# Graph attention kernel: a row bent by VectorE before one exponential, first-row steps inside the leftover loop, minus x in earlier batches

## What is computed

```
s = HW @ a[:OUT_F, 0]
t = HW @ a[OUT_F:, 0]
e = jax.nn.leaky_relu(s[row] + t[col], negative_slope=ALPHA)
m = jax.ops.segment_max(e, row, num_segments=N_NODES)
ex = jnp.exp(e - m[row])
den = jax.ops.segment_sum(ex, row, num_segments=N_NODES)
att = ex / den[row]
agg = jax.ops.segment_sum(att[:, None] * h[col], row, num_segments=N_NODES)
```

## Time and profile before

| | us |
|---|---|
| median of 3 runs | 394.81 |
| the 3 runs | 394.67, 394.81, 396.28 |
| profiled execution, its own time | 394.77 |
| its span | 393.0 |

### The profile page before, as it was taken

The page is one execution under the profiler, slowest core; times in us unless marked ns, Lnnn a source line. Parts: engine busy times, 40 slices in busy tenths (PEclk is TensorE's granted clock), DMA queues, the critical chain, the costliest instruction groups (busy, mean ns, idle before and its releaser), DMA issues.

```text
span 393.0 us, 5049 instructions
## 1 busy us (share of the span) xinstructions
PE 379.8 (97%) x1888; PEld 299.6 (76%) x1888; DVE 346.1 (88%) x438; ACT 261.4 (67%) x251; POOL 35.3 (9%) x88
## 2 busy tenths in 40 slices
PE   5999979999999999999999999999999999999994
PEld 2556647888888888778888888888888888888883
DVE  8999989986787698999899999889999899989445
ACT  1569964755566879865786766777758686866222
POOL 5000310000000001001010101001010101001000
PEclk9999999999999999999999999999999999999999
DMA  7900891000000036549545464623423453633202
GB/s 251 391 16 2 141 274 62 3 0 0 2 0 2 0 108 224 151 127 322 167 123 182 124 166 156 203 66 89 127 60 100 130 170 128 224 92 87 75 27 101
DMA packets 23482, 45.90 MB, mean 117 GB/s; under 512 B 1862, under 2 KB 2074, under 8 KB 23458
## 3 DMA queue, kind: packets, MB, share of 16 engines
q0 software_dynamic: 12400, 24.00, 23.2%
q1 hardware_dynamic: 11058, 21.58, 16.4%
HBM read 43.02 MB, written 2.56 MB: 116 GB/s over the span
## 4 chain that ended last, share of the span: by engine, by line
PE 90%; ACT 5%; DMA 2%; DVE 1%; issue 1%; SPq 0%; DVEq 0%
PE PS L1237 63%; PE PS L1177 17%; PE PS L1115 3%; PE PS L1158 3%; DMA av<-in_a 2%; ACT C L857 2%; PE PS L1045 1%; PE PS L1187 1%; ACT xl L884 1%; ACT Z L862 1%; PE PS L1063 1%; PE PS L1101 1%; PE PS L1095 0%; ACT strow L850 0%; ACT ex L902 0%
## 5 line engine op out<-in xcount | busy, mean ns | idle before, releaser
L1237 PE MATMUL PS<-wh,s 128*128 128x512 f32 x720 | 222.8, 390 | 0.4 <-issue 0.4
L1237 PEld LDWEIGHTS PS<-wh,s 128*128 128x128 f32 x720 | 135.1, 188 | 29.7 <-issue 1.8
L1237 PE MATMUL PS<-wl,s 128*128 128x512 f32 x360 | 140.1, 389 | 0.0
L1237 PEld LDWEIGHTS PS<-wl,s 128*128 128x128 f32 x360 | 67.6, 188 | 13.9
L966 ACT ACTIVATE s<-v 128x1280 fp32r<-128x1280 f32 (+1 forms) x32 | 40.0, 1251 | 40.6 <-DVE v L775 23.8
L949 ACT ACTIVATE v<-xt,bias 128x1280 f32<-128x1280 f32 (+1 forms) x32 | 42.9, 1340 | 20.1 <-DVE s L785 18.7
L769 DVE SCALAR_TENSOR_TENSOR v<-v,v 128x1280 f32<-128x1280 f32 (+1 forms) x32 | 46.4, 1450 | 6.3 <-ACT v L952 6.3
L775 DVE SCALAR_TENSOR_TENSOR v<-v,v 128x1280 f32<-128x1280 f32 (+1 forms) x32 | 46.8, 1461 | 3.7 <-DVE v L771 0.5
L785 DVE SCALAR_TENSOR_TENSOR s<-v,s 128x1280 fp32r<-128x1280 f32 (+1 forms) x32 | 46.5, 1454 | 2.4 <-ACT s L966 2.4
L425 POOL DMA_DIRECT2D wh<-in_splT x32 | 22.9, 715 | 272.2 <-PE PS L1237 172.5
L771 DVE SCALAR_TENSOR_TENSOR v<-v,v 128x1280 f32<-128x1280 f32 (+1 forms) x32 | 46.5, 1453 | 0.0
(11 more groups left out here) (141 smaller groups left out, 347.8 us busy)
## 6 DMA issues: line engine op xcount, KB each, us to landing
wh<-in_splT POOLq DMA_DIRECT2D x32, 512.0 KB, 4.2
wring<-in_splT SPq DMA_DIRECT2D x21, 512.0 KB, 4.0
xt<-in_xT SPq DMA_DIRECT2D x1, 2500.0 KB, 12.3
xh<-in_x POOLq DMA_DIRECT2D x1, 2304.0 KB, 11.6
out<-xr SPq DMA_DIRECT2D x9, 256.0 KB
wh<-in_baseT POOLq DMA_DIRECT2D x4, 512.0 KB, 5.2
xl<-in_x POOLq DMA_DIRECT2D x1, 1536.0 KB, 11.9
wring<-in_baseT SPq DMA_DIRECT2D x3, 512.0 KB, 4.6
```

The lines of the kernel that those rows point to most:

```text
L1237: m = e.matmul(PS[:, w % 8, :], sx[:, ic, tl * 128:tl * 128 + 128], wx[:, ic, :], start=first and n == 0, stop=last and n == 2)
```

## The change

Four things are changed.

1. **One exponential per row tile.** ACT writes a new tile `gentle`, 0.2 times `trow`, once (`e.mul`, ahead of all exponentials). Of the two exponentials and the maximum behind them, DVE now takes the maximum first: `bent(j)` is the greater of `gentle - s_part` and `trow`, in one instruction per row; ACT then takes one exponential of it in place (`grow`), and `weigh` is the product with `C` alone. `small` has three one-column instructions, the first two of which do not wait for each other.
2. **Steps moved into the loop's body.** The marks of windows 22 to 24 are split: row tiles 0 and 1 (`NEAR`) inside the loop, ahead of the addition to `C`; the other eight behind `weigh(1)`. The second part of row tile 0's greatest value and `bent(0, 0)` stand in the body as well. The wait for `top` moves from the end of the body to the start of a turn and to the instruction behind the loop.
3. **Minus x** is written in batches 6 to 15, not 8 to 17.
4. **Orders.** On DVE `greatest(1)` goes behind both pieces of row tile 0's `weigh`, and each `bent(j)` stands between `greatest(j)` and `small(j)`, up to j = 3; from 4 on it stands behind `p_low(j - 2)`. PE's zero matmuls are 6 and 2 in place of 8, 4, 4 and 2, and both turns of row tile 0 stand ahead of its sums.

```diff
-        NEGATIVE_AT = {8 + k: k for k in range(NT)}
+        NEGATIVE_AT = {6 + k: k for k in range(NT)}
-        MARKED, MARKED_AHEAD = 20, 22
+        MARKED, MARKED_AHEAD, NEAR = 20, 22, 2
...
+            e.memset(top[:, 0:LW], -BIG).then_inc(s_touch, 1)
...
+            def bent(j, p=0):
+
+                lo, hi = pieces(j)[p]
+                if j >= 3:
+                    e.wait_ge(s_t, upto(j - 3, len(pieces(j - 3)) - 1))
+                e.wait_ge(s_trow, 3)
+                e.wait_ge(s_scol, 3)
+                e.wait_ge(s_gentle, 1)
+                return e.scalar_tensor_tensor(out=ex[:, j % 3, lo:hi], in0=gentle[:, lo:hi], scalar=s_part[:, j:j + 1],
+                                              in1=trow[:, lo:hi], op0=ALU.subtract, op1=ALU.max)
...
+                    e.wait_ge(s_touch, n + 1)
                     greatest_of(0, slice(0, DW * MARKED), LW).then_inc(s_early, 1)
                     e.wait_ge(s_cnt, taken(MARKED_AHEAD - 1))
                     marks(MARKED, MARKED_AHEAD).then_inc(s_ahead, 1)
+                    e.wait_ge(s_cnt, len(TAKEN))
+                    marks(MARKED_AHEAD, ND, 0, NEAR).then_inc(s_near, 1)
...
+                    greatest_of(0, slice(DW * MARKED, N), LW + 1).then_inc(s_late, 1)
                     e.wait_ge(s_ova, n + 1)
+                    e.wait_ge(s_late, n + 1)
...
-                    e.wait_ge(s_touch, n + 1)
-            marks(MARKED_AHEAD, ND).then_inc(s_marked, 1)
-            e.wait_ge(s_marked, 1)
+                    bent(0, 0).then_inc(s_first, 1)
...
-                e.wait_ge(s_e1, n)
-                e.wait_ge(s_e2, n)
-                e.tensor_tensor(b, b, ex[:, 3, lo:hi], ALU.max).then_inc(s_top, 1)
-                e.wait_ge(s_top, n)
+                e.wait_ge(s_ex, upto(j, p))
...
             small(0)
+            bent(0, 1).then_inc(s_z, 1)
+            weigh(0, 0)
+            weigh(0, 1)
             greatest(1)
-            weigh(0, 0)
+            bent(1).then_inc(s_z, 1)
             small(1)
-            weigh(0, 1)
             p_low(0, 0)
+            p_low(0, 1)
+            weigh(1)
+            marks(MARKED_AHEAD, ND, NEAR, NT).then_inc(s_marked, 1)
+            e.wait_ge(s_marked, 1)
             greatest(2)
...
+            def grow(j, p=0):
...
+                e.wait_ge(s_small, smalls(j + 1))
+                e.activation(b, b, ACT.Exp, bias=sm[:, 1, j:j + 1]).then_inc(s_ex, 1)
...
+            e.mul(gentle[:, :], trow[:, 0:N], SLOPE).then_inc(s_gentle, 1)
```

More of the change, by code:

```diff
@@ L186, in build @@
         s_setup = sem("s_setup")
-        (s_reach, s_bits, s_col, s_mk, s_bound, s_left, s_tab, s_mv, s_head, s_ovk, s_ovm, s_ovs, s_ova, s_ovz, s_marked, s_ahead, s_early, s_touch, s_late, s_tmax, s_small, s_top, s_p, s_den, s_rden, s_plo,
+        (s_reach, s_bits, s_col, s_mk, s_bound, s_left, s_tab, s_mv, s_head, s_ovk, s_ovm, s_ovs, s_ova, s_ovz, s_marked, s_ahead, s_early, s_near, s_touch, s_first, s_late, s_tmax, s_small, s_z, s_p, s_den, s_rden, s_plo,
          s_a3, s_b3, s_spl, s_slo, s_wlo, s_res, s_bns, s_bna, s_rstd, s_nb, s_fin) = (
             sem(f"v_{n}") for n in (
-                "reach", "bits", "col", "mk", "bound", "left", "tab", "mv", "head", "ovk", "ovm", "ovs", "ova", "ovz", "marked", "ahead", "early", "touch", "late", "tmax", "small", "top", "p", "den", "rden", "plo",
+                "reach", "bits", "col", "mk", "bound", "left", "tab", "mv", "head", "ovk", "ovm", "ovs", "ova", "ovz", "marked", "ahead", "early", "near", "touch", "first", "late", "tmax", "small", "z", "p", "den", "rden", "plo",
                 "a3", "b3", "spl", "slo", "wlo", "res", "bns", "bna", "rstd", "nb", "fin"))
-        (s_lk, s_sq, s_neg, s_war, s_wa, s_srow, s_trow, s_scol, s_cnt, s_hole, s_e1, s_e2, s_phi, s_ya, s_ev, s_abs, s_q2, s_a2,
+        (s_lk, s_sq, s_neg, s_war, s_wa, s_srow, s_trow, s_scol, s_cnt, s_hole, s_gentle, s_ex, s_phi, s_ya, s_ev, s_abs, s_q2, s_a2,
          s_silu, s_shi, s_root, s_fina) = (sem(f"a_{n}") for n in (
-             "lk", "sq", "neg", "war", "wa", "srow", "trow", "scol", "cnt", "hole", "e1", "e2", "phi", "ya", "ev", "abs", "q2", "a2",
+             "lk", "sq", "neg", "war", "wa", "srow", "trow", "scol", "cnt", "hole", "gentle", "ex", "phi", "ya", "ev", "abs", "q2", "a2",
              "silu", "shi", "root", "fina"))
@@ L600, in _ @@
                     e.wait_ge(s_tab, TABLE)
-                    first, tiles, first_win, many = (
-                        within(v, *ends) for v, ends in zip(loaded(e, r_size, 0, 4, 0, LND * NC), (
-                            (0, NC), (1, NC + 1), (0, LND - 1), (1, LND))))
+                    first, tiles, first_win, many, left = (
+                        within(v, *ends) for v, ends in zip(loaded(e, r_size, 0, 5, 0, LND * NC), (
+                            (0, NC), (1, NC + 1), (0, LND - 1), (1, LND), (1, LND * NC))))
             def greatest_of(j, d, k):
@@ L670, in greatest @@
                 if j == 0:
-                    greatest_of(0, slice(DW * MARKED, N), LW + 1).then_inc(s_late, 1)
-                    e.wait_ge(s_late, 1)
+                    e.wait_ge(s_touch, left + 1)
                     e.tensor_reduce(tmax[:, 0:1], top[:, :], AX.X, ALU.max).then_inc(s_tmax, 1)
@@ L746, in _ @@
             inverse(2)
+            greatest(3)
+            bent(3).then_inc(s_z, 1)
             small(3)
@@ L751, in _ @@
                 p_low(j + 1)
+                if j + 3 < NT:
+                    bent(j + 3).then_inc(s_z, 1)
                 if j + 2 < NT:
@@ L979, in scale @@
                                  ).then_inc(s_fina, 1)
-            for p in range(2):
-                e1(0, p)
-                e2(0, p)
+            e.wait_ge(s_trow, 3)
+            e.mul(gentle[:, :], trow[:, 0:N], SLOPE).then_inc(s_gentle, 1)
+            grow(0, 0)
+            grow(0, 1)
             p_high(0, 0)
-            e1(1)
-            e2(1)
             p_high(0, 1)
+            grow(1)
             p_high(1)
-            e1(2)
-            e2(2)
+            grow(2)
             normalise(0)
-            e1(3)
+            grow(3)
             for j in range(1, NT - 1):
@@ L1192, in _ @@
             e.wait_ge(s_tmax, 1)
[L1193 to L1197 removed]
+            keep_warm(6)
+            e.wait_ge(s_ex, 1)
+            keep_warm(2)
             turn(0, 0)
[L1199 removed]
+            turn(0, 1)
             sums(0, 0, 0)
[L1201 removed]
             sums(0, 2, 0)
@@ L1204, in _ @@
             sums(0, 2, 1)
+            sums(0, 1, 0)
             turn(1)
-            sums(0, 1, 0)
             sums(0, 1, 1)
```

58 lines of the change are left out of this document (18 added, 40 removed).

## The result

| us | kernel before | changed kernel |
|---|---|---|
| runs beside each other | 11, median 394.97 (394.64 to 396.4) | 11, median 394.05 (394.0 to 394.63) |
| ratio | | 0.9968, 95% interval 0.9956 to 0.998 |
| the profiled execution, its own time | 394.77 | 394.55 |
| its span | 393.0 | 392.7 |

The forecast was 393.7, with a range of 392.6 to 395.1 and "within 0.5%" at 0.85. The time came in the range and in that class, 0.35 above the forecast. A gain of 0.9 stands against a forecast of 1.05, but it is not made of what the prediction said.

A forecast was written before the change was run, and what follows sets the result against it. DVE's work in the handoff from counting to row tiles was taken to hold PE: 0.58 of DVE plus 0.47 that was to spare gave 1.05, so 394.77 - 1.05 = 393.7, with 8 in 10 between 392.6 and 395.1.

The forecast's parts named there:

- within 0.5%: Whole kernel: a time within about 2.0 us of no change, between 392.8 and 396.8, chance 0.85.
- What bounds: Handoff from counting to row tiles, 46 to 60 us: DVE is late, not ACT; PE later waits for row tile 2's ph.
- Minus x: gain nil: Last counts: ACT ready about 0.7 earlier, but two row tiles' marks take the place of DVE's 0.31 wait; addition near 48.63.
- The loop's body: Steps up to tmax: the 0.43 of branches runs beside bent(0, 0), so tmax starts at 50.72 instead of 51.30, gain 0.58.
- DVE's stretch from `tmax` to row tile 3's bias: DVE's list after tmax: added and removed steps sum to +0.1 or nothing, so 20.1 us again and the bias at 70.8.
- From the bias to the exponential: ACT at row tile 3: bias before at 71.4, exponential from 71.45; now the bias comes 0.58 earlier, at 70.8.
- From the exponential to PE: Exponential 1.25, copy 1.21, ph at 73.3; PE starts sums(2, 0) at 73.3 to 73.4, not 74.38: gain 1.05.
- PE ahead: Row tile 0: PE idles 1.75 before tmax, transposes at 52.9 and 54.1, 3.0 us ahead; 1.9 turns into a wait.
- The clock at nothing: Handoff: with fewer zero matmuls the granted clock still holds, as through the longer pause before; cost nothing.
- The rival's own reckoning: Clock falls in the handoff: PE has about 0.9 in hand before the gain suffers; 395.8, up to 400, chance 0.06.
- The 0.40 at 161.87 moves with PE: Near the end of the row tiles: PE's 0.40 us break hangs on row tile 9's ACT and DVE work and shifts with PE.

The follow-up runs named there:

- the changed kernel with the clock up: Changed kernel with 16 zero matmuls in place of 8 ahead of the wait for tmax: median 394.04, lowest 394.02.
- the swap alone: Kernel before with row tile 2's ph copy put ahead of row tile 3's first exponential on ACT: ratio 1.0005, lowest 394.71; profiled execution 396.82.
- the shifted list: Kernel before with nine one-column memsets of a spare tile in DVE's setup: 394.52 in one run; with 17 zero matmuls too, median 394.51, lowest 394.46.
- one swap in ACT's list: Changed kernel with row tile 2's ph copy put ahead of row tile 3's exponential: median 393.3, lowest 392.85, ratio 0.9945.
- all 36 timed runs: Runs of four kernels, made from the kernel before or the changed kernel, with 16 or 17 zero matmuls in place of 8 ahead of tmax; medians 392.81 to 394.81.

## Why the prediction was right in the time, and not in its parts

The steps, held against the changed kernel with the clock up (counting from 4.95, so no correction is needed).

- **What bounds.** Right. The path ran through DVE in the handoff, then through row tile 3's bias, its exponential and row tile 2's `ph`. PE's idle time before `sums(2, 0)` was foreseen, place and releaser. That only the handoff decides was wrong: the 0.40 at 162 and the row tiles between, below.
- **Minus x: gain nil.** Right for the sum as made (the addition at 48.71, foreseen 48.63); xl's last DMA landed 11.3 after its start at 42.7, at 54.0, foreseen near 54, against a first use at 56.21.
- **The loop's body.** The order worked as foreseen, the branches are hidden. `tmax` came at 50.91, foreseen 50.72. The missing 0.19 is 0.08 at the addition (the marks of 300 took 0.24 in the one trace that shows them apart; I had taken 0.22, and the line through the two rows gives 0.19), 0.07 in the steps up to `top`, and 0.04 because `bent(0, 0)` is an instruction with a column operand, costed at the price of one with a constant.
- **DVE's stretch from `tmax` to row tile 3's bias.** Foreseen 20.1, measured 20.06 (50.91 to 70.97). The size is right with errors in it that cancel: `bent(3)` cost 1.44 to the next start and not 1.39, the wait for the second piece's exponential 0.44 and not 0.30, and row tile 0's two `pl` 0.08 more than before; against that, the gaps behind the maxima gave 0.26 and not 0.12 (with the dearer `bent` taken off already), the wait ahead of row tile 2's product 0.45 and not 0.36, and the four `small` 0.04 more than put down. That these come out even is luck.
- **From the bias to the exponential: the step that failed most plainly.** I read before's bias at 71.39, its fourth one-column step, and had the exponential start at 71.45 from it. The row of ACT names L692 as its releaser, the third step, which started at 71.20; L695 served only the second exponential. In the changed kernel L707 is the last step and all there is. From the start of the releasing step to the exponential both take 0.25 (71.20 to 71.45, 70.97 to 71.23). So 0.19 of the gain at the bias was never there. The name in that row's bracket, which the prediction itself shows, would have told it.
- **From the exponential to PE.** 1.24 and 1.21 as foreseen, but PE starts 0.15 behind the end of the copy (in the changed kernel the chain has "issue" of 0.14 there), not at once. Sum: 0.19 at `tmax`, 0.19 at the bias and 0.15 here make 0.53, less 0.02 to 0.04 in the stretch; foreseen gain at `sums(2, 0)` 1.05, measured 0.55 (74.38 less 73.83).
- **PE ahead.** Its pause before `tmax` was to be 1.75; 2.40 less the 0.58 would have been 1.82, and it was 2.02 in the changed kernel's trace, where `tmax` came 0.37 earlier. Foreseen 3.0, measured 2.5 at the last group of products ahead of the wait (71.63 before, 69.13 now): the transposes came at 53.27 and 54.57, foreseen 52.9 and 54.1.
- **The clock at nothing.** Wrong as a statement of hardware, right as a term. "Before, the clock held through the longer pause" rested on one execution; in about half of the kernel before's it did not, and it fell in the profiled one and in four more of the 11 runs of the changed kernel. The rival's own reckoning, that PE has some time in hand before a lower clock costs anything, is what saved the term: PE was 1.07 late at the first transposes, its wait for row tile 2's `ph` was shorter by 0.67, and nothing arrived behind it. The Trainium skill ("TensorE: Matmul & The Clock Gate", "What's actually happening") has activity release the throttle; the traces agree in part: the lower level came behind PE's pauses of 2.01, 2.02, 2.44 and 2.53 in four profiled executions, and did not behind 2.40 (before), 2.32, 2.14, 1.97 and 1.79, nor behind any of 0.33 to 0.41.
- **"The 0.40 at 161.87 moves with PE."** Wrong for this change. Where DVE's list is unchanged it does: with the swap alone, in the kernel before, PE came 1.87 later to row tile 3's transposes and the pause stood at 163.95. In the changed kernel it went away. What the shifted list shows is that it depends on which instructions stand ahead of it in DVE's list.

Put together, by spans: 0.55 from the handoff, less 0.16 in six row tiles and 0.04 up to 148, and 0.40 at 162, is 0.75, and the span of before less that of the changed kernel with equal start and clock is 0.8 (393.0 and 392.2). By lowest times it is 0.64 (394.64 and 394.0). So of a gain of 0.6 to 0.8, some 0.2 (0.40 less 0.16 and 0.04) has nothing to do with the change's purpose, and that the time came within 0.35 of the forecast owes something to luck. The rest of the difference of medians comes from the share of before's runs in which the clock fell.

Why the hold at 162 and the 0.03 per row tile exist stays open. The idea in the expectations, a fetch of instructions in blocks, fits the 320th entry and the packets of the instruction queue; that the fetch is the cause no run here shows.

## What to carry to other kernels

Where a step's start is to be moved, take the releaser's name from the waiting engine's own row, not the last instruction of the group that feeds it; here the wrong one of two neighbours cost a fifth of the forecast. When one engine gets early, look for the first instruction of another that sits in order behind a wait it doesn't need: one swap in ACT's list was worth more (1.15 by the lowest times) than the whole change (0.64). And before a small gain is believed, shift the program's instructions by a few that do nothing: here that alone moved the time by 0.2 to 0.3. Where the mean granted clock of each timed run is on record, sort the runs by it first: here it told the two groups apart, where one trace did not.

## What the runs showed of the hardware

- A pause of PE of 2.0 to 2.5 us in a busy stretch lets the granted clock fall to 0.50 for some 3 us in some executions of the same kernel and not in others; with the pause filled to 0.4 the mean granted clock was 0.996 or more in all 36 timed runs. In the kernel before the fall costs 1.4 in about half of the runs; in the changed kernel, which has a wait of PE behind it, nothing.
- A column of scalars as third operand of a DVE instruction over two tensors costs 0.06 us more than a constant, at 512, 738 (0.99 against 0.93) and 1,250 columns.
- A DVE instruction was held for 0.35 us behind its own wait, as the 320th entry of DVE's list in all three traces of kernels where it has that place; nine one-column memsets some 156 us earlier removed it, and the time fell by 0.2 in 12 runs.
- The counting starts at 4.95 or 5.46 in executions of the changed kernel, and stays that much late to the end (span 392.2 and 392.7); in five traces of the kernel before and its variants it was 4.95 or 4.96.
